# Last projection in four column tiles, last half inverse copied inside SBUF, at most two map loads in flight

## The chip, the cores and the metric

The kernel runs on one core of a Trainium2 chip. The metric is the time in microseconds (us) of one execution on the device; a kernel's time is the median of several executions. A profiled execution is one of them that the hardware profiler recorded, and runs a little longer.

## The reference, cut to what matters

The input x is 64 images of 64 x 64 points. A Fourier neural operator turns them into token maps, and one transformer block follows.

```python
h = concat([x, gx, gy]); v = h @ p_w + p_b             # 32 channels, 64 images, 64 x 64 points
for i in range(4):
    x_ft = rfft2(v)                                    # 24 kx (low and high) x 12 ky are kept
    out1 = einsum('bixy,ioxy->boxy', x_ft[:, :, :12, :12], W1)
    out2 = einsum('bixy,ioxy->boxy', x_ft[:, :, -12:, :12], W2)
    v = irfft2(modes of out1, out2) + conv1x1(v, w_w[i]) + w_b[i]
    v = batchnorm(v) * bn_g[i] + bn_b[i]               # over all images and points
    if i < 3: v = relu(v)
h = v @ q_w + q_b                                      # 64 x 64 tokens x 64 features
h = concat([cls_tok, h])                               # 65 tokens
h = h + attn(layernorm(h))                             # linear attention, 8 heads of 8, norms of k and v
h = h + moe(layernorm(h))                              # 8 experts, top 2
```

## The kernel before, in words

Four images are a quad; 16 quads make the batch. The work before the change's place is three passes over the quads (layers 0 to 2). A pass of layer l computes each quad's output map (`out_set`, L1620), stores it in `maps_d` or keeps it, and already transforms it for the next layer (`y_transform`, `x_transform`; L1678, L1690). Between the passes lies `mix(l)`: TensorE multiplies the kept modes with the layer's complex weights, six weight tiles of which GpSimd loads (L1243) and half negates (L1249) at the start of the mixing; ScalarE copies and squares the products, VectorE sums them for the batch norm.

The last layer has no pass of its own. The last batch norm and the projection `q_w` are linear, so its output is projected at once. The output of the projection, 64 images of 64 x 64, is the sum of two parts, and both are accumulated in PSUM banks 0 to 3 on TensorE:

- the *stream*: for each quad a map of 128 partitions x 4096 (2 MB) of layer 2's output, multiplied by a 128 x 32 matrix cut out of `placed` (L1752): eight matmuls of 512 columns, each recorded twice. The quads come in the order `CONSUMED`; k counts them. k = 0 and 1 are still in SBUF (`KEPT`), the other fourteen are loaded from DRAM by SP (`stream_load`, L1211) into seven buffers (`slot(k)`). `fin_full` counts the maps that have been consumed; it frees the buffers for k = 7 and up. k = 2 and 3 are loaded into the buffers that the pass read its inputs from, k = 4 into the tile `turned`, k = 5 and 6 over the modes.
- the *last inverse transform*: after `mix(3)` the modes are projected with `mode_q` (L1720, L1725), copied to SBUF by ScalarE (L1468, L1470), written to DRAM and read back in another layout by GpSimd (L1326, L1331, L1337; `kl_in`), and transformed along x by TensorE after map k = 3 (L1763). ScalarE copies the result to `x_last` (L1473; `xl_ev`). GpSimd stores `x_last` to the DRAM tensor `line_d` (L1342; `xl_st`), and GpSimd and ScalarE load it back with four transfers each as `g_last` (`last_tile`, L1099; `gl_in`). `last_inverse(c)` (L1740) multiplies it into the banks.

The batch is in two halves, c = 0 for quads 0 to 7 and c = 1 for quads 8 to 15. A half's lines lie at partitions 64 h + 32 c of all four banks, so one map's matmuls alternate between two groups of 32 output columns, 64 h apart. The first eight maps consumed are c = 0. After k = `EARLY` = 9 TensorE waits for both `gl_in` and does `last_inverse(0)`, then the rest of the stream, then `last_inverse(1)`.

Behind it ScalarE evacuates the first half in eight pieces (L1480; `bank_ev`), GpSimd stores it to `tok_d` (`store_lines`, L397) and loads it back with tokens on partitions (`group_load`, L403; `tok_st`). VectorE then works through the first norms of this group (`first_norms(1)`, L682 to L708). ScalarE takes the roots in it (`first_root`, L428, L431; roots 0 and 1 are those of the class token, 2 and 3 those of the first group), and evacuates the second half only after root 3 (L1487). SP stores and loads that half. VectorE's chain of first group, second group, second norms, router, experts and TensorE's matmuls between them then goes to the end.

Every engine and each DMA queue works in the order written: SP's queue, ScalarE's and GpSimd's take an instruction only when the wait before it is met.

Of the kernel before, what the change touches and what calls it, by code (L numbers as in the profile page):

```python
# [6 lines left out]
KX_HALF, KY = 12, 12  # L7
# [105 lines left out]
def tower_kernel(nc, images, p_rows, p_cols, mode_w, conv_w, conv_t, layer_cols, q_cols, cls_tok, head_rows,  # L113
# [13 lines left out]
    line_d = dram("projected_half", [KY, 2, 4, 16, BATCH])  # L127
# [3 lines left out]
    with ctx:  # L131
# [113 lines left out]
        gtile = [t.rearrange("p (x n) -> p x n", x=16) for t in (take(2048), *xhalf[0:2])]  # L245
# [42 lines left out]
        kl_in, xl_full, xl_ev, xl_st, gl_in = sem("kl_in"), sem("xl_full"), sem("xl_ev"), sem("xl_st"), sems("gl_in")  # L288
# [197 lines left out]
        def tensor_tokens(pe):  # L486
# [36 lines left out]
            pe.wait_ge(bank_ev, 12)  # L523
# [592 lines left out]
        def _(sp):  # L1116
# [85 lines left out]

            for l in range(PASSES):
# [6 lines left out]
            def stream_load(k):  # L1210
                sp.dma_start(stream[slot(k)], maps_d[PASSES - 1, CONSUMED[k]]).then_inc(stream_in[slot(k)], 16)  # L1211

            for s in range(2):
                sp.wait_ge(map_st[s], stores(PASSES, 0))
            for pair in range(2):
                sp.wait_ge(a_full[pair], PER_PASS * PASSES)
            stream_load(2)
            stream_load(3)

            sp.wait_ge(x2_ev, mode_of(LAYERS - 1, 6) + 1)  # L1220
            stream_load(4)
# [10 lines left out]
            sp.wait_ge(bank_ev, 12)  # L1232
            store_lines(sp, 1)
            sp.wait_ge(line_st[1], 32)
# [6 lines left out]
        def _(pool):  # L1241
# [107 lines left out]
            pool.wait_ge(line_st[0], 32)  # L1349
# [6 lines left out]
        def _(act):  # L1356
# [128 lines left out]
            for g in range(4):  # L1485
                act.wait_ge(bank_full, g + 5)
# [660 lines left out]
```

## Time and profile before

| | us |
|---|---|
| runs | 1375.55, 1375.92, 1376.15 (median 1375.92) |
| profiled execution | 1386.14 |
| its span, first to last instruction | 1384.3 |
| mean granted TensorE clock | 0.920 of full speed |
| TensorE busy | 1146.5 (83%) |
| VectorE busy | 855.8 (62%) |
| ScalarE busy | 552.4 (40%) |
| GpSimd busy | 365.1 (26%) |

The span is cut by stage rather than by engine: the stream and the last inverse lie between 1160 and 1226, the tokens' chain after that. Times in rows are us from the span's start. A line of a DMA transfer in a queue (SPq, ACTq, POOL with DMA_DIRECT2D) is its issue; the landing comes later.

### The profile page before, as it was taken

What the parts mean: (1) busy time and instruction counts of PE and PEld (TensorE: products, weight loads), DVE (VectorE), ACT (ScalarE), POOL (GpSimd) and SP (SyncE); (2) the same over time, 40 slices, a digit from 0 to 9 for tenths busy, and PEclk for the clock granted to TensorE, in tenths of its full rate; (3) what the DMA queues carried; (4) which work ended last, traced back from release to release, by engine and by line L of the source; (5) the groups of instructions that cost most, each with busy time, mean ns of one, the idle gap of its engine ahead of it and who ended that gap; (6) DMA issues with size and microseconds to landing.
All of it is one profiled execution on the core that took longest, in us unless ns stands there. A gap on an engine that the chain in (4) does not pass through costs nothing.

```text
span 1384.3 us, 40498 instructions
## 1 busy us (share of the span) xinstructions
PE 1146.5 (83%) x18183; PEld 656.8 (47%) x18183; DVE 855.8 (62%) x1033; ACT 552.4 (40%) x808; POOL 365.1 (26%) x525
## 2 busy tenths in 40 slices
PE   3659899999969899899896989889899767954697
PEld 3434555555544455555454445445455452323552
DVE  6547566777648566676664857656666661058664
ACT  2136344445436434344443654434344462100150
POOL 6384212121336301212123730121212261100000
PEclk9779799999989999999998999999999989976788
DMA  6268998898517899999981789999999176931001
GB/s 161 53 185 223 250 271 210 212 226 207 141 46 199 219 331 347 311 353 326 334 248 36 204 217 347 326 317 334 306 338 291 23 269 240 388 119 37 2 0 31
DMA packets 154711, 300.29 MB, mean 217 GB/s; under 512 B 32552, under 2 KB 98488, under 8 KB 137604
## 3 DMA queue, kind: packets, MB, share of 16 engines
q1 hardware_dynamic: 131418, 251.63, 60.2%
q0 software_dynamic: 20864, 45.32, 11.7%
q8 instruction: 143, 2.34, 0.7%
q10 hardware_dynamic: 2256, 0.75, 0.2%
q14 instruction: 30, 0.25, 0.1%
HBM read 147.86 MB, written 128.48 MB: 200 GB/s over the span
## 4 chain that ended last, share of the span: by engine, by line
PE 55%; DMA 16%; DVE 12%; ACT 5%; issue 5%; SPq 4%; POOL 2%; ACTq 0%; DVEq 0%; POOLq 0%
PE ps L1616 13%; PE ps L1655 11%; DMA inputs<-maps 7%; PE ps L1678 6%; PE ps L1690 6%; PE ps L1641 4%; PE ps L1579 3%; PE ps L1543 3%; DMA half_inverse<-arena 2%; PE ps L1558 1%; PE ps L1529 1%; SPq L1053 1%; ACT arena L1427 1%; PE ps L624 1%; DMA arena<-arena 1%
## 5 line engine op out<-in xcount | busy, mean ns | idle before, releaser
L1655 PEld LDWEIGHTS ps<-arena 48*128 48x128 f32 x3072 | 191.2, 197 | 84.6 <-issue 84.6
L1655 PE MATMUL ps<-arena 48*128 48x128 f32 x3072 | 211.6, 289 | 5.0 <-issue 2.9
L1427 ACT ACTIVATE arena<-ps,arena 128x1024 f32<-128x1024 f32 x96 | 112.3, 1202 | 229.8 <-PE ps L1655 208.0
L1094 POOL DMA_DIRECT2D arena<-arena x207 | 120.9, 591 | 304.2 <-ACT arena L1444 300.9
L1436 ACT ACTIVATE ps<-ps 128x1024 f32<-128x1024 f32 x144 | 145.5, 1011 | 111.1 <-PE ps L1616 110.9
L2067 DVE STREAM_TRANSPOSE arena<-ps 128x1024 f32<-128x1024 f32 x96 | 177.3, 1929 | 2.2 <-PE ps L1678 2.2
L1616 PE MATMUL ps<-arena 32*32 32x512 f32 x2944 | 158.5, 620 | 8.0 <-issue 4.9
L1678 PE MATMUL ps<-arena 32*32 32x512 f32 x3072 | 152.8, 616 | 8.0 <-issue 4.6
L2054 DVE STREAM_TRANSPOSE arena<-arena 128x2048 f32<-128x2048 f32 x64 | 144.4, 2289 | 18.6 <-issue 10.0
L1690 PE MATMUL ps<-arena 128*64 128x96 f32 x2304 | 123.4, 258 | 33.4 <-DVE arena L2067 27.8
L1690 PEld LDWEIGHTS ps<-arena 128*64 128x64 f32 x2304 | 103.9, 142 | 89.0 <-issue 51.1
L1249 POOL TENSOR_SCALAR arena<-arena 32x384 f32<-32x384 f32 x96 | 112.9, 1176 | 83.6 <-DMA arena<-in_mode_w 77.3
L2029 DVE TENSOR_SCALAR arena<-ps,arena 128x1024 f32<-128x1024 f32 x32 | 43.0, 1344 | 128.4 <-PE ps L1655 128.4
L1616 PE MATMUL ps<-inputs,arena 32*32 32x512 f32 x1920 | 106.2, 613 | 16.5 <-DMA inputs<-maps 8.5
L1543 PE MATMUL ps<-arena 64*64 64x64 f32 x2304 | 79.7, 287 | 42.4 <-DMA arena<-arena 39.1
L1543 PEld LDWEIGHTS ps<-arena 64*64 64x64 f32 x2304 | 65.1, 154 | 91.8 <-issue 78.6
L1427 ACT ACTIVATE inputs<-ps,arena 128x1024 f32<-128x1024 f32 x48 | 56.1, 1202 | 117.8 <-PE ps L1655 95.5
L1243 POOL DMA_DIRECT2D arena<-in_mode_w x48 | 27.2, 573 | 267.8 <-ACT arena L1444 257.0
L2038 DVE BATCH_NORM_STATS2 arena<-ps 128x6 f32<-128x512 f32 x96 | 62.3, 690 | 43.7 <-PE ps L1616 43.7
L2054 DVE STREAM_TRANSPOSE arena<-inputs 128x2048 f32<-128x2048 f32 x32 | 72.7, 2313 | 8.2 <-issue 4.0
L1034 ACT COPY arena<-ps 128x1024 f32<-128x1024 f32 x66 | 56.2, 857 | 51.4 <-PE ps L1579 51.4
L1616 PEld LDWEIGHTS ps<-arena 32*32 32x32 f32 x2944 | 39.4, 104 | 77.7 <-ACT arena L1427 28.4
(314 smaller groups left out, 1393.9 us busy)
## 6 DMA issues: line engine op xcount, KB each, us to landing
arena<-half_inverse SPq DMA_DIRECT2D x90, 384.0 KB, 12.1
half_inverse<-arena SPq DMA_DIRECT2D x120, 256.0 KB, 4.5
maps<-arena SPq DMA_DIRECT2D x112, 256.0 KB, 4.5
maps<-inputs SPq DMA_DIRECT2D x112, 256.0 KB, 10.2
arena<-maps SPq DMA_DIRECT2D x28, 1024.0 KB, 16.0
maps<-arena SPq DMA_DIRECT2D x28, 1024.0 KB, 19.1
inputs<-maps SPq DMA_DIRECT2D x28, 1024.0 KB, 25.3
arena<-in_mode_w POOLq DMA_DIRECT2D x48, 384.0 KB, 7.2
```

The lines of the kernel that those rows point to most:

```text
L1094: eng.dma_start(dst, src).then_inc((modes_st[batch % 2], last_st, late_st)[part], 16)
L1249: nc.gpsimd.tensor_scalar(w, w, -1.0, None, ALU.mult).then_inc(signed, 1)
L1427: nc.scalar.activation(half(h_out(l, q), h)[:, 1024 * pair:1024 * pair + 1024], ps[:, 2 * pair:2 * pair + 2, :].rearrange("p b n -> p (b n ...
L1436: nc.scalar.activation(src, src, ACT.Square, accum_out=sums_x2[:, i:i + 1])\
L1543: last = nc.tensor.matmul(ps[64 * e:64 * e + 64, 2 * s + m, 0:384] .rearrange("p (b k) -> p k b", b=BATCH)[:, k], ring[2 * p + e][rows, 6 ...
L1616: last = nc.tensor.matmul(ps[32 * x:32 * x + 32, r, :], w[rows, 32 * r:32 * r + 32], source[rows, at:at + 512], start=True, stop=last_one)
L1655: last = nc.tensor.matmul(ps[:, b, at:at + 128], gtile[s][rows, 4 * b + 2 * h + n, :], iy[rows, :], start=False, stop=(i >= 2 and n == 1))
L1678: last = nc.tensor.matmul(ps[32 * x:32 * x + 32, 4 + r, :], fyt[rows, yh, :], src, start=(yh == 0), stop=(yh == 1))
L1690: last = nc.tensor.matmul(ps[64 * t:64 * t + 64, 4 + b, 96 * (y - 3 * b):96 * (y - 3 * b) + 96], spectra[:, at:at + 64], fx2[:, r, :], sta ...
L2038: last = nc.vector.bn_stats(stats[:, 12 * q + 6 * b:12 * q + 6 * b + 6], ps[:, 2 + b, :])
L2054: nc.vector.transpose(dst, src).then_inc(h_turned, 1)
L2067: nc.vector.transpose(dst, src).then_inc(y_turned, 1)
```

## The change

The stream and the last inverse change, and the order of loads on SP. No other function changes.

- `line_of(c, g, h)` gives each of a half's eight lines one of four groups of 32 output columns and one of two banks: half 0 uses banks 0 and 1, half 1 banks 2 and 3. A map's eight matmuls now rotate over four column groups. The evacuation of a half is two instructions of 128 partitions; the store of a half is four transfers for two. The second half is evacuated after roots 0 and 1 and before roots 2 and 3.
- `line_d` is gone. `last_tile` copies from `x_last` to `g_last` directly: twelve transfers for t = 0 from GpSimd and twelve for t = 1 from ScalarE, each of 64 partitions x 64 numbers to 4 partitions x 1024.
- L1763's transform is done after map k = 5 (was 3), and `last_inverse(0)` after k = 10 (was 9).
- Map loads k = 2, 3 and 4 are issued in the last pass, as soon as their buffers are free, before SP's share of the copies of the spectra (`place_part`). The scratch tile of the last mixing moves from `turned` to a tile of its own to make room. From k = 7 on a load also waits until the load two before it has landed.

```diff
-            for h in range(2):
-                rows = slice(64 * h + 32 * c, 64 * h + 32 * c + 32)
-                eng.dma_start(tok_d[32 * c:32 * c + 32, h:8:2, :], lines[rows].rearrange("p (g n) -> p g n", g=4))\
+            for r in range(4):
+                eng.dma_start(tok_d[32 * c:32 * c + 32, r:8:4, :],
+                              lines[32 * r:32 * r + 32, 1024 * c:1024 * c + 1024].rearrange("p (g n) -> p g n", g=2))\
                    .then_inc(line_st[c], 16)
...
-        EARLY = 9
+        EARLY = 10
...
+        def line_of(c, g, h):
+
+            at = 32 * (2 * (g % 2) + h)
+            return slice(at, at + 32), 2 * c + g // 2
...
         def last_tile(eng, t):
 
-            for r in range(4):
-                eng.dma_start(g_last[64 * t + r:64 * t + 4 * KY:4], line_d[:, t, r]).then_inc(gl_in[t], 16)
+            eng.wait_ge(xl_ev, 1)
+            for ky in range(KY):
+                row, at = 64 * t + 4 * ky, 64 * (KYH * (ky % 2) + ky // 2)
+                eng.dma_start(g_last[row:row + 4].rearrange("r g b -> r (g b)").rearrange("r (g b) -> r g b", g=16),
+                              x_last[64 * t:64 * t + 64, at:at + 64]).then_inc(gl_in[t], 16)
...
+                if l == PASSES - 1:
+                    for s in range(2):
+                        sp.wait_ge(map_st[s], stores(PASSES, 0))
+                    for k in range(KEPT, 4):
+                        for pair in range(2):
+                            sp.wait_ge(a_full[pair], set_of(l, "out", QUADS - 4 + k, 1) + 1)
+                        stream_load(k)
+                    sp.wait_ge(y_full, QUADS * PASSES)
+                    stream_load(4)
                 sp.wait_ge(xs_ev, 2 * QUADS * (l + 1))
                 place_part(sp, l, LAST, 2, 2, 1)
...
             for k in range(7, QUADS):
                 sp.wait_ge(fin_full, k - 6 if k < 11 else k - 5)
+                sp.wait_ge(stream_in[slot(k - 2)], streamed(k - 2))
                 stream_load(k)
...
-            pool.wait_ge(xl_ev, 1)
-            for e in range(2):
-                pool.dma_start(line_d.rearrange("(y e) t r g b -> e (t r g) y b", e=2)[e],
-                               x_last[:, 384 * e:384 * e + 384].rearrange("p (y b) -> p y b", b=BATCH))\
-                    .then_inc(xl_st, 16)
-            pool.wait_ge(xl_st, 32)
             last_tile(pool, 0)
-            pool.wait_ge(bank_ev, 8)
+            pool.wait_ge(bank_ev, 2)
             store_lines(pool, 0)
...
-            act.wait_ge(xl_st, 32)
             last_tile(act, 1)
             act.wait_ge(q_read, 2)
-            for g in range(4):
-                act.wait_ge(bank_full, g + 1)
-                for rows in (slice(0, 32), slice(64, 96)):
-                    nc.scalar.activation(lines[rows, 512 * g:512 * g + 512], ps[rows, g, :], ACT.Identity,
-                                         bias=qbias[rows]).then_inc(bank_ev, 1)
-            for i in range(4):
+            for c in range(2):
+                act.wait_ge(bank_full, c + 1)
+                for b in (2 * c, 2 * c + 1):
+                    nc.scalar.activation(lines[:, 512 * b:512 * b + 512], ps[:, b, :], ACT.Identity, bias=qbias)\
+                        .then_inc(bank_ev, 1)
+                if c == 0:
+                    for i in range(2):
+                        first_root(act, i)
+            for i in range(2, 4):
                 first_root(act, i)
-            act.wait_ge(line_st[0], 32)
-            ...
...
-                        b = 64 * h + 32 * (q // 8)
-                        last = nc.tensor.matmul(ps[b:b + 32, g, :], placed[:, 60 - 4 * (q % 8):92 - 4 * (q % 8)],
+                        rows, b = line_of(q // 8, g, h)
+                        last = nc.tensor.matmul(ps[rows, b, :], placed[:, 60 - 4 * (q % 8):92 - 4 * (q % 8)],
                                                 stream[slot(k)][:, at:at + 512], start=(k % 8 == 0), stop=False)
                 last.then_inc(fin_full, 1)
-                if k == 3:
+                if k == 5:
...
-                tile = spectra if l < PASSES else turned
+                tile = spectra if l < PASSES else last_scratch
```

`last_inverse(c)` does the same 32 matmuls, in two turns of 16 for four of 8, with its outputs placed by `line_of`.

## Rows read from the trace of the kernel before

**Rows 1.** Chain of waits, 1176 to 1232: start us, us, what; a DMA piece is the flight.

```profile
1177.22 1.57 PE ps L1763 x4
...
1180.68 0.81 ACT arena L1473
...
1182.64 7.25 DMA projected_half<-arena
...
1192.02 0.75 ACTq L1099
...
1192.79 8.70 DMA arena<-projected_half
...
1201.63 1.55 PE ps L1740 x48
...
1203.26 0.68 ACT arena L1480
...
1209.15 0.54 POOL token_maps L397
1209.69 10.04 DMA token_maps<-arena
...
1220.59 0.84 POOL arena L403
1221.42 4.28 DMA arena<-token_maps
...
1229.71 1.23 DVE arena L686
```

**Rows 2.** Timeline, PE: start us, us, engine line op out<-in xcount [idle before <-releaser].

```profile
1159.90 0.62 PE L1752 MATMUL ps<-arena 128*32 128x512 f32 x1
...
1180.57 17.07 PE L1752 MATMUL ps<-arena 128*32 128x512 f32 x80
```

**Rows 3.** Windows: stretch, us, PE PEld DVE ACT POOL busy, PEclk, DMA share, GB/s.

```profile
1110.00:1112.00 2.00, 0.00 (x0) 0.00 (x0) 0.00 (x0) 0.00 (x0) 0.64 (x2) 0.50 0.80 169
1165.00:1175.00 10.00, 9.66 (x44) 2.62 (x41) 0.00 (x0) 0.00 (x0) 2.39 (x4) 1.00 0.98 325
1205.00:1215.00 10.00, 10.00 (x48) 2.68 (x46) 3.23 (x16) 4.24 (x8) 1.11 (x2) 1.00 1.01 427
```

**Rows 4.** Timeline, weight loads of L1720 at full clock (four column groups).

```profile
1156.43 0.12 PEld L1720 LDWEIGHTS ps<-arena 128*32 128x32 f32 x4 [0.35 <-issue]
1156.86 0.12 PEld L1720 LDWEIGHTS ps<-arena 128*32 128x32 f32 x4 [0.31 <-issue]
```

**Rows 5.** Line L1243 (weights), landing times: layer 2's mixing, then layer 3's.

```profile
DMA to landing us min/median/max: 4.7/6.2/7.2
...
DMA to landing us min/median/max: 9.2/14.0/15.0
```

**Rows 6.** Timeline, PE, mixing of layer 3.

```profile
1129.97 1.54 PE L1543 MATMUL ps<-arena 64*64 64x64 f32 x48 [1.97 <-POOL arena L1249]
```

**Rows 7.** Landing times of L397; L1094 at 200 to 370; L1094 at 900 to 1060.

```profile
DMA to landing us min/median/max: 3.5/6.5/10.0
...
DMA to landing us min/median/max: 5.7/6.1/7.5
...
DMA to landing us min/median/max: 7.1/11.9/21.0
```

**Rows 8.** DMA queues (packets, MB, share): 1209:1220 twice, 1247.5:1253, 1189.8:1202 (ScalarE's).

```profile
q1 hardware_dynamic: 244, 3.47, 74.2%
q0 software_dynamic: 160, 0.52, 11.7%
...
q1 hardware_dynamic: 2383, 0.78, 69.5%
...
q10 hardware_dynamic: 96, 0.20, 4.6%
```

**Rows 9.** Line L1211 (map loads), landing times.

```profile
DMA to landing us min/median/max: 7.9/11.9/18.8
```

More of the change, by code:

```diff
@@ L242, in tower_kernel @@
         stats = take(12 * QUADS)
-        gtile = [t.rearrange("p (x n) -> p x n", x=16) for t in (take(2048), *xhalf[0:2])]
+        last_scratch = take(2048)
+        gtile = [t.rearrange("p (x n) -> p x n", x=16) for t in (last_scratch, *xhalf[0:2])]
         x_pair = [view(at, 4096).rearrange("p (e n) -> p e n", e=2)
@@ L287, in tower_kernel @@
         xl_real = sem("xl_real")
-        kl_in, xl_full, xl_ev, xl_st, gl_in = sem("kl_in"), sem("xl_full"), sem("xl_ev"), sem("xl_st"), sems("gl_in")
+        kl_in, xl_full, xl_ev, gl_in = sem("kl_in"), sem("xl_full"), sem("xl_ev"), sems("gl_in")
         stream_in, fin_full = sems("stream_in", 7), sem("fin_full")
@@ L1201, in layer_pass, with stream_load @@
                         g_load(l, i + 3)
+            def stream_load(k):
+                sp.dma_start(stream[slot(k)], maps_d[PASSES - 1, CONSUMED[k]]).then_inc(stream_in[slot(k)], 16)
             for l in range(PASSES):
@@ L1205, in _ @@
                 layer_pass(l)
+                if l == PASSES - 1:
[7 more added lines that the diff above has]
+                    stream_load(4)
                 sp.wait_ge(xs_ev, 2 * QUADS * (l + 1))
                 place_part(sp, l, LAST, 2, 2, 1)
[L1210 to L1221, printed above, removed]
             sp.wait_ge(x2_full, mode_of(LAYERS - 1, KY - 1) + 1)
@@ L1231, in _ @@
             sp.wait_ge(fin_full, QUADS)
-            sp.wait_ge(bank_ev, 12)
+            sp.wait_ge(bank_ev, 4)
             store_lines(sp, 1)
-            sp.wait_ge(line_st[1], 32)
+            sp.wait_ge(line_st[1], 64)
             group_load(sp, 1)
@@ L1473, in _ @@
             nc.scalar.copy(x_last.rearrange("p (b n) -> p b n", b=2), ps[:, 5:7, 0:384]).then_inc(xl_ev, 1)
-            act.wait_ge(xl_st, 32)
             last_tile(act, 1)
             act.wait_ge(q_read, 2)
-            for g in range(4):
-                act.wait_ge(bank_full, g + 1)
-                for rows in (slice(0, 32), slice(64, 96)):
-                    nc.scalar.activation(lines[rows, 512 * g:512 * g + 512], ps[rows, g, :], ACT.Identity,
-                                         bias=qbias[rows]).then_inc(bank_ev, 1)
-            for i in range(4):
-                first_root(act, i)
-            act.wait_ge(line_st[0], 32)
-            for g in range(4):
-                act.wait_ge(bank_full, g + 5)
-                nc.scalar.activation(lines[:, 512 * g:512 * g + 512], ps[:, g, :], ACT.Identity, bias=qbias)\
-                    .then_inc(bank_ev, 1)
+            for c in range(2):
[7 more added lines that the diff above has]
+            for i in range(2, 4):
+                first_root(act, i)
             scalar_tokens(act)
@@ L1730, in last_inverse @@
             def last_inverse(c):
-                for i, turn in enumerate(TURNS):
-                    if i >= 2:
-                        pe.wait_ge(turn_done, 4 * QUADS * PASSES + 2 * c + i - 1)
+                for turn in range(2):
+                    if turn:
+                        pe.wait_ge(turn_done, 4 * QUADS * PASSES + c + 1)
                     for n in range(2):
-                        for half_x, g in turn:
-                            rows = slice(64 * half_x, 64 * half_x + 48)
-                            at = 256 * n + 128 * half_x
+                        for low in range(2):
                             for h in range(2):
-                                b = 64 * h + 32 * c
-                                last = nc.tensor.matmul(ps[b:b + 32, g, at:at + 128],
-                                                        g_last[rows, 4 * g + 2 * h + n, 32 * c:32 * c + 32],
-                                                        iy[rows, :], start=False, stop=(i >= 2 and n == 1))
-                    last.then_inc(bank_full if i >= 2 else turn_done, 2 if i >= 2 else 1)
+                                for half_x in range(2):
+                                    g = 2 * ((turn + half_x) % 2) + low
+                                    rows = slice(64 * half_x, 64 * half_x + 48)
+                                    at = 256 * n + 128 * half_x
+                                    line, b = line_of(c, g, h)
+                                    last = nc.tensor.matmul(ps[line, b, at:at + 128],
+                                                            g_last[rows, 4 * g + 2 * h + n, 32 * c:32 * c + 32],
+                                                            iy[rows, :], start=False, stop=(turn == 1 and n == 1))
+                    last.then_inc(bank_full if turn else turn_done, 1)
             for k, q in enumerate(CONSUMED):
@@ L1769, in _ @@
                     for t in range(2):
-                        pe.wait_ge(gl_in[t], 64)
+                        pe.wait_ge(gl_in[t], 16 * KY)
                     last_inverse(0)
```

5 lines of the change are left out of this document (2 added, 3 removed).

## The prediction

> **What bounds the kernel now.** I read the chain of waits over the end of the program first. The reader is to see that the last third of it does not hang on matmuls: it is one chain of small transfers [rows 1]. TensorE transforms the last spectra (L1763), ScalarE copies them out, GpSimd stores them in DRAM, and the 256-byte pieces come back by eight transfers (L1099; ScalarE's last lands at 1201.49). Then come the last inverse of the first half (L1740), eight evacuations, a store of the token maps and their load; VectorE starts the first group's norms at 1225.7. From there VectorE's own chain leads to the end, so the change is worth what it does to 1225.7 plus whatever holds VectorE later.
>
> TensorE's row over the same stretch looks like a bound but is none: 80 records (five maps of 16) in 17.07 us, 3.4 us a map, back to back [rows 2]. The second half's maps are evacuated only after ScalarE's root for the first group, at 1239, so TensorE's end at 1226.2 has 13 us of room. The transfers of the maps are the other busy resource: 427 GB/s with all DMA engines full; 2.10 MB / 427 = 4.9 us a map [rows 3].
>
> **The change part by part.** Times below are of the profiled execution, whose span of 1384.3 lies in 1386.14; the runs shown have a median of 1375.92, so I add the difference in us to that.
>
> *Column tiles.* Before, a map's eight matmuls alternate between two column groups and go at 2 records per 0.43 us (17.07/80 = 0.213 each). L1720 rotates over four groups with the same shape and goes at 4 records per 0.43 us [rows 2, 4]. So a map costs 1.7 us, not 3.4; the bounds are 1.7 and 3.4. Sixteen maps save 27 us of TensorE, off the path. What is late next is the transfers: nine maps (k=7 to 15) must be loaded after the first is consumed.
>
> *Maps 2 to 4 loaded earlier.* They go out at about 1075 to 1097, into idle DMA engines, not at 1111.7 beside the weights of the last mixing. The weights' landings were 9.2 to 15.0 us there and 4.7 to 7.2 us one layer earlier [rows 5], without that company. GpSimd's sign flips then start some 4 us earlier, and TensorE's waits for them go: 1.97 us [rows 6] and a second of 0.8. ScalarE (2.4 us a mode) and VectorE take over; following them mode by mode I get 1.4 us (bounds 0 and 2.8). SP's six small transfers now stand behind three loads, which have landed by 1104 and the copies start at 1107: nothing. The scratch tile moved away costs nothing.
>
> *Until the last transform.* The stream starts at 1159.9 - 1.4 = 1158.5, the first map is consumed at 1160.6 and the first load flows from 1161.8, some 3 us earlier than before. It meets GpSimd's stores of the projected modes, and I let that eat the 1.4: L1763 again at 1177.2 (bounds 1175.5 and 1179). TensorE has then been idle since about 1169, though, and such a gap leaves the granted clock at 0.50, the 1.2 GHz level [rows 3]; 3.4 us of transform become some 5.2. The copy (0.8) ends at 1183.3.
>
> *The half inverse copied on the chip.* Removed: L1342 and its 7.25 us, then eight gathers. Added: 12 transfers of 64 pieces of 256 bytes on GpSimd and 12 on ScalarE. Issue alone: 12 x 0.75 = 9.0 us on ScalarE [rows 1], to 1192.3. If they landed as the quickest transfer of the token maps does, 3.5 us after its issue [rows 7], they would be in at 1196, 5 us before 1201.5. But they run beside the loads, for which the nearest rows say three things. (a) L397's 160 packets from GpSimd are 10 on each of 16 engines, and took 0.54 + 10.04 = 10.6 us beside the loads, where the same store from SP on idle engines took 3.5 and some more (I take 4.2) [rows 1, 7, 8]: 6.4 us for 10 packets, 0.64 a packet, which is the time of one 16 KB packet of a load (3.47 MB in 244 packets with the completions; 16.4 KB at 427/16 GB/s = 0.61 us). So each packet of another queue waits for one packet of the loads, whatever its size. (b) L1094's identical copies land in 5.7 to 7.5 us in the first layer's pass and 7.1 to 21.0 in the third, where the transfers beside them have longer rows [rows 7]. (c) GpSimd's queue gathers pieces (0.52 MB in 160 packets), a sequencer's hardware queue does not: the token gather of 256-byte pieces made 2383 packets of 0.78 MB. And ScalarE's 4 transfers of L1099, 12 outer rows each, made 96 packets: 12 of data and 12 completions each, so as many engines as outer rows [rows 8]. The new ones write 4 rows: by that pattern 4 engines, with 16 + 1 packets per transfer on each, 12 x 17 = 204. At 0.64 us that is 130 us as long as loads flow; when they end, packets of that queue go at 0.026 us (69.5% of 16 engines over 5.5 us, by 2383 [rows 8]).
>
> So the copies land shortly after the loads end. Loads: 1161.8 + 9 x 4.9 = 1205.9; plus 3 for the gather of the projected modes (325 in place of 427 GB/s over ten us [rows 3] is 2.4) and 2 for the copies themselves: 1211 (bounds 1206 and 1214). By then (1211 - 1187) / 0.64 = 38 of 204 packets are through, 166 x 0.026 = 4.3 are left, and with the completion gl_in is there at 1216. GpSimd's twelve, gathered, are in at about 1198 and don't decide.
>
> The page "DMA: Bandwidth & Descriptors" of the Trainium skill says in "Queues, rings and completion order" that an engine takes turns between queues packet by packet, with 9 to 17 descriptors typical in a packet. Here ScalarE's and SP's small packets were one piece each (330 bytes on average), so (c) decides over "typical"; what it would give otherwise is the third rival.
>
> *Limit of two loads.* A load waits for the one two before it; with one still queued behind, SP's queue runs dry nowhere (a load lands 7.9 us after its issue at the least, 4.9 of them its own flow [rows 9]). The copies meet the same row of 16 KB packets: nothing; bounds -1 and +2 us on the loads' end. Behind that wait on SP stands only cls_tok, which is not due.
>
> *After the copies.* TensorE has waited since about 1191, its clock is low: last_inverse(0) 1.6 becomes 3.2. Evacuation: 2 of 0.68 for 8, saving 4.1 us. Four stores for two: 0.3 + 3 x 0.55 until the last goes out, then 4.2 us, since the loads are over, in place of 10.04. Load: 0.3 + 0.84 + 4.3. Sum 0.1 + 3.2 + 1.4 + 0.3 + 1.65 + 4.2 + 0.3 + 0.84 + 4.3 = 16.3, so VectorE starts at 1216 + 16.3 = 1232.3, 6.6 us later than 1225.7.
>
> *ScalarE's order.* Roots 2 and 3 now stand behind the second half's evacuation. TensorE does k=11 to 15 and the inverse from 1219.3: 5 x 1.7 + 1.8 cold + 2 = 1231.6, evacuated at 1233. VectorE wants root 2 at its start + 5.2 [rows 1] = 1237.5: hidden, 4 us to spare. Behind VectorE's start nothing changes.
>
> **Forecast: 1375.9 + 6.6 = 1382.5 us.** Own range 1377 to 1388.
>
> **Rivals.**
> 1. *The copies get through beside the loads* (many small packets per turn). gl_in at 1197 to 1199 (issue end plus the landing of GpSimd's); inverse and evacuation to 1203; last store out 1205, 8 to 10 us beside loads: 1214; load to 1219.5, root 2 in time. 6 us earlier plus up to 2: 1368. For it: a 256-byte packet occupies an engine for hardly anything; against it: the completions in (a) are 4-byte packets and count as full turns.
> 2. *Turns, but the loads end early or the copies spread over 16 engines* (12 x 5 = 60 packets, 22 left at 1211): gl_in at 1212, VectorE 2.6 later: 1378; with the loads ending at 1207, 1374.5 to 1376. Same or barely slower. For it: ends of my bounds; against: the 12-engine pattern.
> 3. *ScalarE's queue packs 16 pieces into a packet, as GpSimd's does* [rows 8]: 12 x 2 = 24 turns x 0.64 = 15 us and 3 to begin: gl_in 1202, store out 1209, beside the last loads 6 us, load: 1220.5, so 1371.
> 4. *The column tiles bring nothing* (3.4 us a map): the loads then follow TensorE as before, ending near 1215 to 1218, and root 2 waits behind the second half: 1384 to 1390.
>
> **Chances.** Forecast 0.40; rival 1 0.25; rival 2 0.20; rival 3 0.10; rival 4 0.05. Range for 8 in 10: 1366 to 1387. A measurement tells about 0.2% (2.75 us) from no change. Faster (below 1373.2): rivals 1 and 3 and little else, 0.36. Same: most of rival 2 and the lower end of the forecast, 0.20. Slower: 0.44.
>
> **What would show it.** Right: L1752 at about 0.11 us a record with TensorE idle between maps; ScalarE's copies issued in 9 us but landing more than 15 us after their last issue, together with the end of the maps' transfers; the chain of waits with one long DMA piece from ScalarE's copies to L1740. Its queue should hold about 816 packets (12 x 68) in that stretch. Wrong: L1740 of the first half before 1200 means turns don't cost what I say; 960 packets mean 16 engines; a wait of VectorE for ScalarE's L428 of several us means that the second half's evacuation stands in the way; records of L1752 still 0.21 apart refute the first part.

## The result, and the profile after

The kernel after takes 1387.03 us (median of 4 runs, 1385.08 to 1387.49), the kernel before 1375.74 beside it; the ratio is 1.0077, 95% interval 1.0042 to 1.0112. Taken again on another occasion the same kernel gave 1.0066 [1.0030, 1.0103]. Ratios leave out executions that ran over 1.5% above the fastest of their kernel.

It is slower, as forecast and by the forecast mechanism, but by more than the 6.6 us forecast: the medians differ by 11.3 us, and 1387.03 lies above the 1382.5 forecast, at the upper end of the forecast's own range of 1377 to 1388 and just over the one given for 8 in 10, to 1387. The profiled execution took 1385.08 us with a span of 1383.2; it is the shortest of the four, where that of before, 1386.14, is longer than all of its runs.

The spans of two profiled executions can't be subtracted here: before's own span (1384.3) is longer than after's. What is compared below is counted from the first matmul of the last mixing, which is at 1113.43 in before and at 1105.81 in after.

The chain of waits of after (start us, us, what), which answers to [rows 1]:

```profile
1153.43 6.92 DMA projected_modes<-arena
...
1171.44 2.94 PE ps L1764 x4
...
1177.38 0.81 ACT arena L1475
1178.21 1.13 ACTq L1106
...
1182.98 5.58 ACTq L1106
...
1188.59 7.34 ACTq L1106
...
1197.14 16.11 DMA arena<-arena
...
1213.39 1.18 PE ps L1741 x32
...
1215.88 1.27 ACT arena L1481 x2
...
1217.44 1.54 POOL token_maps L396 x3
1218.98 2.71 DMA token_maps<-arena
...
1222.81 4.75 DMA arena<-token_maps
1227.59 1.23 DVE arena L682
```

From the copy of the transform's result (L1475) to the last inverse (L1741) it is 36.0 us: of ScalarE's twelve issues two stall ahead of the last, for 5.58 and 7.34 us, and the last copy lands 16.11 us after its issue began. In [rows 1] the same way, by DRAM, ended at 1201.63, 21 us after its copy began (in the second trace of before, c1, 23.2 us). Behind it the chain is quick: store 2.71 us (10.04 before), since no load is left to run beside it.

TensorE over the same stretch, answering to [rows 2], with ScalarE's issues between (start us, us, engine line op out<-in xcount [idle before <-releaser]):

```profile
1150.77 3.57 PE L1753 MATMUL ps<-arena 128*32 128x512 f32 x28
1153.79 0.60 PE L1753 MATMUL ps<-inputs,arena 128*32 128x512 f32 x2
...
1171.44 5.90 PE L1764 MATMUL ps<-arena 24*128 24x384 f32 x8 [9.80 <-DMA arena<-projected_modes]
...
1178.21 24.73 ACTq L1106 DMA_DIRECT2D arena<-arena  x12
...
1213.39 2.33 PE L1741 MATMUL ps<-arena 48*32 48x128 f32 x64 [25.64 <-DMA arena<-arena]
```

28 records start between 1150.77 and 1153.79, 0.108 us apart at full clock, against 0.211 by the same measure in before (80 between 1180.57 and 1197.48): the column tiles work. The maps of one stretch run back to back, as the window shows (columns as in [rows 3]):

```profile
1155.00:1160.00 5.00, 5.00 (x52) 1.63 (x48) 0.00 (x0) 0.00 (x0) 0.00 (x0) 1.00 0.85 293
```

TensorE's idle time lies ahead of the transform (9.80 us) and of the last inverse (25.64 us). All twelve issues of ScalarE together take 24.73 us.

DMA queues between 1178 and 1214 (packets, MB, share of 16 engines), and the landing times of all fourteen map loads (L1212) and of the weights (L1251) in the last mixing, to [rows 8], [rows 9] and [rows 5]:

```profile
q1 hardware_dynamic: 782, 10.48, 83.6%
q10 hardware_dynamic: 816, 0.20, 3.5%
q0 software_dynamic: 384, 0.21, 2.7%
...
DMA to landing us min/median/max: 7.6/11.1/15.3
...
DMA to landing us min/median/max: 3.2/5.9/7.6
```

ScalarE's queue (q10) holds 816 packets, 12 x 68, as the prediction had it: four engines. The nine loads issued between 1150 and 1215 land in 9.8 to 15.3 us. The weights land in 5.9 us at the median in place of 14.0.

The places in us from the start of the last mixing, from the timelines. "Transform" is the start of L1763 or its equal, "inverse" that of `last_inverse(0)`, VE1 and VE2 the starts of VectorE's first and second group (L682, 128 x 1024), and the last column is the ratio of the times to before, with its 95% interval:

```
kernel                  transform inverse  VE1    VE2    end    ratio
before                     63.8    88.2   112.3  140.0  270.9
c1 before, again           64.6    91.0   114.7  141.2  272.3  1.0032 [1.0000, 1.0063]
after                      65.6   107.6   121.8  149.4  277.4  1.0077 [1.0042, 1.0112]
a1 after, again            69.4   107.2   121.2  148.9  277.0  1.0066 [1.0030, 1.0103]
a2 load 11 held            63.1    80.8   112.2  143.0  273.9  1.0029 [0.9987, 1.0072]
a3 no limit of two         66.6   106.2   120.1  147.9  278.4  1.0045 [1.0000, 1.0090]
a4 column tiles only       67.7    90.2   113.8  139.9  268.2  1.0000 [0.9958, 1.0042]
b1 way by DRAM             63.5    93.0   110.7  138.2  266.4  0.9973 [0.9938, 1.0008]
b2 DRAM, load 10 held      62.8    79.2   114.0  140.1  268.6  0.9974 [0.9941, 1.0007]
b3 copies, load 10 held    65.9    82.5   116.3  142.5  270.7  0.9983 [0.9946, 1.0019]
b4 24 copies on GpSimd     63.4   108.2   122.6  150.4  280.1  1.0054 [1.0018, 1.0090]
c2 early loads only        63.3    89.9   112.9  140.7  269.2  0.9983 [0.9952, 1.0014]
c3 one queue               65.9    82.2    97.4  132.4  260.5  0.9911 [0.9875, 0.9946]
d1 loads in 4 KB pieces    61.8   109.7   123.8  151.6  281.3  1.0075 [1.0040, 1.0110]
```

Before against itself (c1) reads 1.0032, so a ratio alone settles no 3 us; two traces of one kernel agree in these columns to 3 us, but for the transform of a1, which is 3.8 us later than in after. The trace of a4 is of its longest execution, 1391.89 us, where its median is 1374.70.

### The profile page after: what moved, and what is told of

The parts are those of the page before. It is cut to its first block, busy times and chain, and to the rows that moved or that the text cites. A ratio compares the mean times of both kernels' runs of the same rounds, so it can differ in the third digit from the quotient of the medians.

```text
span 1383.2 us, 40517 instructions
## 1 busy us (share of the span) xinstructions
PE 1118.7 (81%) x18183; PEld 645.4 (47%) x18183; DVE 855.6 (62%) x1033; ACT 546.5 (40%) x800; POOL 370.3 (27%) x533
## 4 chain that ended last, share of the span: by engine, by line
PE 59%; DVE 12%; DMA 9%; SPq 6%; ACT 5%; issue 5%; ACTq 1%; POOL 1%; DVEq 0%
PE ps L1615 14%; PE ps L1654 11%; PE ps L1677 7%; PE ps L1689 6%; PE ps L1578 4%; PE ps L1640 3%; PE ps L1542 3%; SPq L1162 2%; DMA arena<-arena 2%; PE ps L1557 2%; DMA arena<-maps 2%; PE ps L1528 1%; ACTq L1106 1%; ACT arena L1429 1%; DVE ps L1907 1%
## 5 line engine op out<-in xcount | busy, mean ns | idle before, releaser
L1654 PEld LDWEIGHTS ps<-arena 48*128 48x128 f32 x3072 | 184.8, 192 | 92.5 <-issue 87.0
L1654 PE MATMUL ps<-arena 48*128 48x128 f32 x3072 | 204.7, 283 | 12.8 <-issue 6.8
L1429 ACT ACTIVATE arena<-ps,arena 128x1024 f32<-128x1024 f32 x96 | 112.3, 1202 | 226.0 <-PE ps L1654 207.4
L1615 PE MATMUL ps<-arena 32*32 32x512 f32 x2944 | 157.3, 624 | 10.0 <-DMA arena<-maps 6.3
L1677 PE MATMUL ps<-arena 32*32 32x512 f32 x3072 | 150.5, 612 | 5.4 <-DVE arena L2055 3.4
L1689 PE MATMUL ps<-arena 128*64 128x96 f32 x2304 | 126.6, 261 | 32.8 <-DVE arena L2068 28.7
L1689 PEld LDWEIGHTS ps<-arena 128*64 128x64 f32 x2304 | 106.7, 145 | 89.9 <-issue 50.7
L1615 PE MATMUL ps<-inputs,arena 32*32 32x512 f32 x1920 | 110.0, 634 | 5.7 <-issue 4.6
L1429 ACT ACTIVATE inputs<-ps,arena 128x1024 f32<-128x1024 f32 x48 | 56.1, 1202 | 119.1 <-PE ps L1654 101.2
L1251 POOL DMA_DIRECT2D arena<-in_mode_w x48 | 27.3, 582 | 262.6 <-ACT arena L1446 252.2
```

What stands on the lines that cost most here:

```text
L1429: nc.scalar.activation(half(h_out(l, q), h)[:, 1024 * pair:1024 * pair + 1024], ps[:, 2 * pair:2 * pair + 2, :].rearrange("p b n -> p (b n ...
L1615: last = nc.tensor.matmul(ps[32 * x:32 * x + 32, r, :], w[rows, 32 * r:32 * r + 32], source[rows, at:at + 512], start=True, stop=last_one)
L1654: last = nc.tensor.matmul(ps[:, b, at:at + 128], gtile[s][rows, 4 * b + 2 * h + n, :], iy[rows, :], start=False, stop=(i >= 2 and n == 1))
L1677: last = nc.tensor.matmul(ps[32 * x:32 * x + 32, 4 + r, :], fyt[rows, yh, :], src, start=(yh == 0), stop=(yh == 1))
L1689: last = nc.tensor.matmul(ps[64 * t:64 * t + 64, 4 + b, 96 * (y - 3 * b):96 * (y - 3 * b) + 96], spectra[:, at:at + 64], fx2[:, r, :], sta ...
```

## The experiments

**a1, after again; a2, the loads held.** a1 is the kernel after unchanged; in a2 SP waits for both `gl_in` before load k=11:

```diff
                 sp.wait_ge(stream_in[slot(k - 2)], streamed(k - 2))
+                if k == 11:
+                    for t in range(2):
+                        sp.wait_ge(gl_in[t], 16 * KY)
```

> The changed kernel once more, beside the runs of before on the same chip, so that the other kernels of this call have their reference. Theory (A: ScalarE's one-piece packets each take a turn with the 16 KB packets of the map loads): 1387 us, first L1741 about 107 us after the first L1542 of the last mixing, as in its first trace (1213.4 - 1105.8), with a wait of some 25 us of TensorE before it. Rival (B: the 11 us lie elsewhere, in noise of the passes): 1376 to 1390 with the tail as before.

> The changed kernel, but SP issues no map load from k = 11 on until both halves of g_last have landed. Theory A: with the load of k = 10 through by about 1182 the copies drain at once; gl_in some 3 us after ScalarE's last issue, at 1190 on the clock of the first trace in place of 1213; the loads of k = 11 to 15 follow from there and end at 1217 (5 x 4.9 plus the store beside them); the store of the first half now runs beside loads (10 us for 4), VectorE starts at 1213 to 1216 in place of 1227.6, root 2 waits 1 to 3 us for the second half: 1373 to 1377 us. Rival B' (24 small transfers are slow by themselves, by their issue and their landing): gl_in no earlier than 1205, the loads end 25 us after it, 1387 us or more.

a1 repeats after to 1 us from the inverse on; its median is 1380.67 us, where I had 1387, with before at 1374.31 beside it. In a2 none of ScalarE's issues stalls (7.62 us for the twelve) and the last copy is in 3.70 us after its issue; then the loads go on. From its chain, and VectorE's wait behind it:

```profile
1176.97 0.56 ACTq L1108
1177.56 3.70 DMA arena<-arena
...
1181.35 8.06 DMA arena<-maps
...
1219.91 1.27 ACT arena L1486 x2
...
1221.40 0.25 DVE L688 RECIPROCAL arena<-arena 128x16 f32<-128x16 f32 x1 [3.38 <-ACT arena L428]
```

The inverse starts 11.7 us after the start of ScalarE's copy (1169.67 to 1181.40), where it was 36.0, so what the copies waited for was the loads. The ratio, 1.0029, separates neither from 1.0 nor from after's: the loads now fall on the first half's stores, and ScalarE's root for VectorE stands behind the second half's late evacuation (L1486), for which VectorE waits 3.38 us. Of what I expected, the inverse came sooner (80.8 from the mixing, where 1190 in after's trace is 84.2), VectorE's start later (112.2, for 107 to 110), and the median of 1379.86 us is above my 1373 to 1377.

**a3, no limit of two.**

```diff
-                sp.wait_ge(stream_in[slot(k - 2)], streamed(k - 2))
```

> The changed kernel without the wait for the load two before. In the trace of the change ScalarE's queue passed most packets in three or four bursts, where SP's queue ran dry between two loads. Theory A: without the limit the queue does not run dry, the bursts go, and ScalarE's copies wait for the end of the loads, which comes 2 to 3 us earlier: gl_in within 3 us of the changed kernel's, 1385 to 1389 us; in a window inside the loads ScalarE's queue makes fewer than 8 packets a us. Rival C (the limit itself costs load time and so the 11 us): 1378 to 1382.

Places within 2 us of after's. The median is 1377.83 us, not the 1385 to 1389 that I expected but the number of rival C; a1, unchanged, has 1380.67 beside it, and the two ratios lie within each other's intervals, so the time doesn't decide between theory and rival. What decides is the inverse at 106.2, no earlier than after's by more than 1.4 us. The queues between 1180 and 1200, a stretch without a burst of q10, and then between 1201 and 1206, where the loads are over:

```profile
q1 hardware_dynamic: 484, 7.11, 97.1%
q0 software_dynamic: 261, 0.14, 2.9%
q10 hardware_dynamic: 118, 0.03, 0.6%
...
q10 hardware_dynamic: 510, 0.12, 13.1%
q1 hardware_dynamic: 21, 0.20, 9.9%
```

118 packets in 20 us on four engines are 4 x 20 / 118 = 0.68 us for each, about the time of one packet of the loads' queue (16 x 20 / 484 = 0.66 us, completions counted with it). 510 of the 816 are left when the loads end, and then take under 5 us. This is the turn of the prediction, measured.

**a4, the column tiles alone.** On before: `line_of`, the new order of `last_inverse`, two evacuations and four stores a half; way by DRAM, loads and EARLY as before.

```diff
-                        b = 64 * h + 32 * (q // 8)
-                        last = nc.tensor.matmul(ps[b:b + 32, g, :], ...
+                        rows, b = line_of(q // 8, g, h)
+                        last = nc.tensor.matmul(ps[rows, b, :], ...
```

> The kernel before with the column tiles alone: line_of, four column groups, two evacuations per half, four stores per half; projected_half in DRAM, the order of the loads, k = 3 and EARLY = 9 and the order of the roots as before. Theory A: L1752 goes at 0.107 us a record, the loads of k = 7 to 10 are issued 2 to 6 us earlier and meet the stores and the gather of the projected modes (+2 to +4), the transform L1763 is at the low clock (+2), the evacuation saves 4: 1375 to 1380 us, so at most a third of the 11 us. Rival D (the column tiles, by starting the loads earlier and cooling TensorE's clock, cost most of it): 1383 or more.

1.0000 [0.9958, 1.0042]: the column tiles with their shorter evacuation show no change by themselves, though the interval can't exclude one of up to 5.8 us either way; VectorE starts at 113.8 (112.3 and 114.7 in before). That rules out rival D, which wanted 1383 us or more; the median is 1374.70.

**b1, the way by DRAM put back.** The reverse cut: after with `line_d`, GpSimd's two stores and 4 + 4 gathers of before; all else stays.

```diff
-            eng.wait_ge(xl_ev, 1)
-            for ky in range(KY):
-                ...
-                eng.dma_start(g_last[row:row + 4]..., x_last[64 * t:64 * t + 64, at:at + 64]).then_inc(gl_in[t], 16)
+            for r in range(4):
+                eng.dma_start(g_last[64 * t + r:64 * t + 4 * KY:4], line_d[:, t, r]).then_inc(gl_in[t], 16)
```

> The kernel after, with the way of the half inverse put back as before (two stores to line_d by GpSimd, then 4 + 4 gathers of 12 x 16 pieces by GpSimd and ScalarE); column tiles, early loads, limit of two and the order of the roots stay. Theory A (the 24 copies are the whole loss, 816 packets of 256 bytes that go one by one beside 16 KB packets): the time from the transform L_x (L1764) to the first last_inverse falls from 42 us to 24 to 28 us as before, VectorE's start of the first group from 121 to 105 to 110 us after the third mixing's start; against the kernel before the total is then lower by what the column tiles' shorter path (before to VectorE's start: some 4 us) and the early loads bring: ratio 0.995 to 0.999. Rival B (the early loads and the limit of two, or the 5.9 us of cold transform, carry a part of the loss): VectorE's start stays 3 us or more behind before's 112 and the ratio above 1.000.

```profile
1170.81 10.49 DMA projected_half<-arena
1181.58 1.54 POOL arena L1107 x3
1183.11 9.48 DMA arena<-projected_half
```

From the start of ScalarE's copy to the inverse the way by DRAM takes 23.8 us beside the same loads (1168.85 to 1192.68; 21.0 and 23.2 in the two traces of before, 36.0 by the copies); VectorE starts at 110.7, 11 us before after, and the ratio falls from 1.0077 and 1.0066 to 0.9973 [0.9938, 1.0008]. The copies are the whole loss; the rest of the change brings VectorE's start 1.6 to 4.0 us forward, which the ratio can't tell from nothing. The inverse is 29.5 us behind the transform's start, above the 24 to 28 expected: the transform itself is 2.2 us longer than before's, the store 3.2.

**b2 and b3, loads held, with either way.** Both hold load k=10 until `gl_in`, set EARLY to 7, and let ScalarE do the four roots ahead of the second evacuation; b2 goes by DRAM, b3 keeps the 24 copies.

```diff
-        EARLY = 10
+        EARLY = 7
...
+                if k == 10:
+                    for t in range(2):
+                        sp.wait_ge(gl_in[t], GL)
...
                 if c == 0:
-                    for i in range(2):
+                    for i in range(4):
                         first_root(act, i)
```

> As b1, and three things more: SP holds the load of map k=10 until the half inverse is in place, the first half's inverse follows map 7 instead of 10, and ScalarE does all four roots of the first group before the second half's evacuation. Theory A (each packet of another queue waits for a 16 KB packet as long as loads flow): bounce in 12 to 14 us after the copy (24 before), VectorE's start at 100 to 106 us after the third mixing's start; the second group's at 128 to 134 (140 before), so 6 to 12 us below before: ratio 0.991 to 0.996. Rival (loads held back come late and the second half is what VectorE waits for): second group not before 138, ratio 0.998 to 1.002.

> The kernel after with the three things of b2 (load k=10 held until the copies are in, first half's inverse after map 7, roots first). Theory A: with no load beside them the 24 copies land within 2 to 4 us after their last issue (11 us after the copy in an earlier run with load 11 held), so gl_in comes at 80 to 82 us after the third mixing's start, VectorE's start 102 to 108, second group 130 to 136; ratio 0.992 to 0.998, within 2 us of b2: the bounce by DRAM costs about as much as issuing twelve copies. Rival (copies on the chip are worth their issue only on idle queues of the chip, and ScalarE's issue of 12 stands in the way of the evacuation): 3 us or more behind b2.

b2's chain, then b3's, then b2's again behind the inverse, where VectorE's start (L683) ends it:

```profile
1167.18 3.06 DMA projected_half<-arena
1170.27 1.30 ACTq L1107
1173.12 2.38 DMA arena<-projected_half
```

```profile
1173.60 0.56 ACTq L1108
...
1174.18 2.68 DMA arena<-arena
...
1177.00 1.18 PE ps L1744 x32
```

```profile
1180.85 12.74 DMA token_maps<-arena
1195.30 15.08 DMA arena<-token_maps
1210.40 1.23 DVE arena L683
```

Beside no load the two ways cost the same: from the end of ScalarE's copy to the inverse 9.6 us by DRAM (1166.03 to 1175.6) and 9.9 by the 24 copies (1167.10 to 1177.00). Copying on the chip saves a store and a gather's latency and gives it back in twelve issues. My expectation for VectorE's start (100 to 108) missed: the loads that were released at the inverse fell on the token maps' store (12.74 us, 2.71 in after) and load (15.08, 4.75 in after). The gain had only been moved along the chain. The rest of my numbers missed with it: the second groups start at 140.1 and 142.5, where I had 128 to 134 and 130 to 136, and the ratios, 0.9974 and 0.9983, are above my ranges (0.991 to 0.996, 0.992 to 0.998). b2's rival had the second group right, but not the reason: it comes 26 us behind the first in both, no more than in before (27.7 and 26.5), so it is the first group that was late.

**b4, all copies on GpSimd.**

```diff
             last_tile(pool, 0)
+            last_tile(pool, 1)
...
-            last_tile(act, 1)
```

> The kernel after with all 24 copies on GpSimd, none on ScalarE. Theory A (turns): a copy of GpSimd's takes about 2 turns on each of 16 engines beside the loads; 24 x 2 x 0.64 = 31 us from 1178, so gl_in comes some 3 to 6 us before after's (104 to 110 us after the third mixing's start) and VectorE's start at 116 to 119; ratio to before 1.000 to 1.006. Rival (the fault is ScalarE's queue of one-piece packets on 4 engines alone; GpSimd's are cheap): gl_in at 95 to 99, VectorE's start at 108 to 112, no slower than before.

```profile
1171.20 14.13 POOL arena L1106 x23
1185.33 23.84 DMA arena<-arena
```

The inverse is at 108.2, no better than after's 107.6. So it isn't ScalarE's queue with its one-piece packets on four engines alone: GpSimd's, with 32 packets a copy on 16 engines (384 for twelve in after) in place of 68 on four, needs as long for 24, and the rival fell. Between 1190 and 1200 GpSimd's queue has 229 packets and the loads' 220, one for one on the same 16 engines, or 0.70 us for each of GpSimd's: the turn again. By turns I had 31 us from the start; measured are 38 (1171.20 to 1209.17), and only then does TensorE go on; VectorE starts at 122.6, later than my 116 to 119.

**c1 and c2, before again and the early loads alone.** c2 is before with SP's part of after for maps 2 to 4 (and the scratch tile moved).

```diff
+                if l == PASSES - 1:
+                    ...
+                        stream_load(k)
+                    sp.wait_ge(y_full, QUADS * PASSES)
+                    stream_load(4)
                 sp.wait_ge(xs_ev, 2 * QUADS * (l + 1))
```

> The kernel before once more, for a second trace. If what is counted from the start of the third mixing is repeatable (theory), VectorE's start of the first group lies again at 112 to 113.5 us from it, the second group's at 140, the end at 268 to 271, whatever the start itself is (1100 to 1120 into the span); ratio 1.000.

> The kernel before with the loads of maps 2 to 4 ahead of the last copies of SP, and nothing else of the change. Theory: the mixing's end comes 1.5 to 2 us earlier (mode_q's matmul at 37 us from the mixing's start, 39 before), but the maps are still consumed at 3.4 us each and their loads follow TensorE, so VectorE's start comes 0 to 2 us earlier: ratio 0.998 to 1.000. Rival: the whole 2 us reach VectorE and the loads of half 1 end earlier too: ratio 0.996 to 0.998.

c1 lies 1 to 3 us over before in each column, VE1 at 114.7 and the end at 272.3 just outside what I wrote. In c2 the first matmul with `mode_q` is at 37.2 (39.0 and 38.4 in before), so the mixing is 1.2 to 1.8 us shorter; 0.9983 [0.9952, 1.0014] can't tell that from nothing.

**c3, no load beside any small transfer.** b2 with load 11 (not 10) held, and the first half's stores and load taken from GpSimd's queue into SP's, ahead of loads 12 to 15:

```diff
+                if k == 11:
+                    for t in range(2):
+                        sp.wait_ge(gl_in[t], GL)
+                if k == 12:
+                    sp.wait_ge(bank_ev, 2)
+                    store_lines(sp, 0)
+                    sp.wait_ge(line_st[0], 64)
+                    group_load(sp, 0)
...
-            pool.wait_ge(bank_ev, 2)
-            store_lines(pool, 0)
-            pool.wait_ge(line_st[0], 64)
-            group_load(pool, 0)
```

> The kernel of b2 (way by DRAM, first inverse after map 7, roots first) with load k=11 held until the half inverse is in place, and the first half's stores and load of token maps put into SP's own queue ahead of loads 12 to 15, so that no load runs beside them. Theory A (a small packet costs one turn of a 16 KB packet only where loads flow): the stores land in 3 to 5 us after the last issue (12.7 in b2), the load of the token maps in 4 to 6 (15.1 in b2), VectorE's start at 94 to 98 us from the third mixing's start (114 in b2, 112 before), and then the second half decides: its tokens land at 126 to 131, so VectorE's second group starts there, 9 to 14 us before before's 140; ratio 0.990 to 0.995. Rival (the loads held back come later than that): second group at 138 or later, ratio 0.997 to 1.000, and VectorE idle for 10 us or more ahead of it.

Its chain, and VectorE's waits for the two groups:

```profile
1180.37 3.07 DMA projected_half<-arena
...
1194.53 4.22 DMA token_maps<-arena
...
1201.10 12.99 DMA arena<-maps
1214.14 9.71 DMA inputs<-maps
...
1203.94 1.22 DVE L683 TENSOR_REDUCE arena<-arena 128x16 f32<-128x1024 f32 x1 [7.29 <-DMA arena<-token_maps]
...
1238.99 1.22 DVE L683 TENSOR_REDUCE arena<-arena 128x16 f32<-128x1024 f32 x1 [1.64 <-DMA arena<-token_maps]
```

0.9911 [0.9875, 0.9946], median 1366.84 us (before 1376.21 beside it): this version beats both kernels. VectorE starts its first group 15 us before before's place and its second 8 us before. The second half, held back behind the pauses, now decides, at 132.4 where I expected 126 to 131.

**d1, the loads in 4 KB pieces.** The turn itself: same bytes, but each map load as four transfers of 128 x 1024.

```diff
-                sp.dma_start(stream[slot(k)], maps_d[PASSES - 1, CONSUMED[k]]).then_inc(stream_in[slot(k)], 16)
+                for j in range(4):
+                    at = slice(POSITIONS // 4 * j, POSITIONS // 4 * (j + 1))
+                    sp.dma_start(stream[slot(k)][:, at], maps_d[PASSES - 1, CONSUMED[k]][:, at])\
+                        .then_inc(stream_in[slot(k)], 16)
```

> The kernel after with each load of a last map (k=2 to 15) written as four transfers of 128 x 1024, so that its pieces and packets are 4 KB in place of 16 KB; the bytes, the limit of two maps and all else stay. Theory A (a small packet of another queue waits for one packet of the loads, so a turn costs 0.16 us here in place of 0.64): 204 packets an engine take at most 33 us and fewer where the queue of SP runs dry, and GpSimd's copies take a quarter: the half inverse is in place 22 to 33 us after its copy (36 in after), 12 to 1 us before the loads end, its issue on ScalarE stalls less (under 5 us in all, 11 in after), VectorE's start 106 to 119 us after the third mixing's start (122), ratio 1.000 to 1.005. Rival (what a small packet waits for has a time of its own, whatever the loads' pieces are): copies in place 35 us after their issue or later, with the end of the loads, ratio 1.006 or more.

Queues between 1180 and 1195:

```profile
q1 hardware_dynamic: 1477, 5.39, 98.6%
q10 hardware_dynamic: 359, 0.09, 2.6%
```

4 x 15 / 359 = 0.167 us for a small packet, and 16 x 15 / 1477 = 0.162 us for one of the loads: with packets of a quarter the turn is a quarter (0.68 in a3). So theory A holds for what a small packet waits for. Its number for the outcome fell, though, and the rival's stood: the inverse came at 109.7 and the ratio is 1.0075. 204 packets at 0.167 are 34 us, about what I had given as the most; the bursts between loads that I had counted on for fewer didn't come (18 to 25 packets a us in each 5 us from 1165 to 1195). The issue on ScalarE stalled as in after, 23.87 us for the twelve, where I had under 5 us of stalls.

## Why the prediction was right, and where it was not

*What bounds the kernel.* Right: the chain of small transfers ahead of VectorE sets the end. The five kernels in which the inverse comes at 106 to 110 have the five highest ratios (1.0045 to 1.0077), and the stream's matmuls show no worth by themselves (a4, 1.0000 within 0.0042).

*Column tiles.* Right: 0.108 a record at full clock for 0.11, off the path. The idle time between maps that I had named as a sign didn't come; TensorE stands idle ahead of the transform and of the inverse.

*Early loads.* Right: `mode_q` starts at 36.99 and 37.17 in after and a1, at 39.03 and 38.42 in before and c1, 1.2 to 2.0 us for 1.4, with the weights' landings as the reason.

*L1763 at the same time.* It came 2 us later (65.6, and 69.4 in a1, for 63.8): the stores of the projected modes took 6.92 us for 2.78, so in this trace their contention ate more than the 1.4. It doesn't always: nine kernels are the same up to this place but for the limit of two in a3, and have it at 62.8 to 69.4, with the same stores at 2.74 us in b1 and 7.17 in c3. Forecasting no change was right within that scatter. I had bounds of 1175.5 to 1179 for it, which are 62.1 to 65.6 from the mixing. The cold transform is 5.90 for 5.2. The window of it (columns as in [rows 3]) has the clock at the 1.2 GHz level, after 9.80 us of idle TensorE:

```profile
1171.00:1177.00 6.00, 5.50 (x8) 2.32 (x8) 0.00 (x0) 0.00 (x0) 0.00 (x0) 0.50 1.00 423
```

*The copies.* The mechanism is shown: small packets wait a load's packet each (a3, b4, d1), the waits vanish when no load flows (a2, b3), and the copies are the whole loss (b1). The step that failed is the one in "Limit of two loads", that SP's queue runs dry nowhere, together with the loads' end at 1211 worked out from 427 GB/s. In after the queues' rows for 1178 to 1183, 1183 to 1185 and 1205 to 1207 are

```profile
q10 hardware_dynamic: 3, 0.00, 0.1%
...
q10 hardware_dynamic: 180, 0.04, 18.5%
...
q10 hardware_dynamic: 252, 0.06, 19.2%
```

and 243 more between 1198 and 1200: 675 of ScalarE's 816 packets went through in three moments of 2 us, not at the end. These are moments in which SP's queue was all but dry. Of the 128 packets of 16 KB of a load, the one before had 22, 4 and 0 left at 1183, 1198 and 1205, and the next had been issued 1.9 to 2.3 us earlier (1180.95, 1196.07, 1202.69); a3 has one such moment as well (150 packets between 1176 and 1178, 9 left at 1176), then 118 packets in 20 us, and 510 at the end. That on the four engines in question the old load was through and the new one not yet there is my reading; the trace doesn't name a packet's engine.

The loads in turn were slower, 10.47 MB between 1178 and 1212 or 308 GB/s, for a reason that no run isolates, and ended at 106 to 107 from the mixing, where I had 1211 or 97.6. The two errors nearly cancel: the inverse at 107.6 for 102.6, 5 us late, and not a drain of 4.3 us behind the loads but under 1. That the forecast of it came so near is in part luck. GpSimd's twelve copies, for which I had 1198 or 84.6, were through at 96, also without effect. The issue on ScalarE, for which I had 9.0 us, took 24.73 (27.08 in a1), with no effect as far as I can see, since the last copies would have waited for the loads anyway; no run tests that.

*Limit of two loads.* Nothing, within the bounds of -1 and +2: a3 is 1 to 2 us earlier at VectorE's start.

*The chain after.* 14.2 us (107.6 to 121.8) for 16.3: the cold inverse took 2.33 for 3.2 and the store 2.71 for 4.2.

*Root 2.* Hidden in after (ScalarE's root for the group waits 4.34 us for VectorE), as forecast; in a2 it was not.

*VectorE's start and behind.* In sum: 121.8 and 121.2, against 112.3 and 114.7, +8.0 on the means, where I had 118.9 (1232.3). Behind it I said nothing changes; before needs 158.6 and 157.7 us from there to the end, after 155.6 and 155.8. So the traces give +5.6 us from the mixing to the end, with 6.6 forecast, at the low end of both intervals (1.0042 and 1.0030 are 5.8 and 4.1 us). The measured ratios give 9 to 11 us. What the rest is, and where the 2.4 us behind VectorE's start come from, stays open; from VE2 to the end traces show 128.0 to 128.5 in eight kernels and 129.7 to 131.1 in six, before among these both times. c2, whose tail is before's, is among the eight, so this part looks like scatter rather than a gain of the change.

The rivals: 1 and 3 needed the inverse before 1200 and fell; so did 4 (0.108 a record). Rival 2's end of the loads was on the wrong side, and the 816 packets mean four engines, not 16. What the Trainium skill says on the page "DMA: Bandwidth & Descriptors", in "Queues, rings and completion order", that engines take turns between queues packet by packet agrees with a3 and d1 (0.68 and 0.167 us a turn); its 9 to 17 descriptors typical in a packet would by my estimate have made 45 to 85 packets of 768 pieces; ScalarE's queue here held 816, one for each piece and completion.

## What to carry to other kernels

Beside a stream of large packets a small transfer paid here per packet, not per byte: count its packets on its busiest engine times the time of one packet of the stream (0.66 us for 16 KB, 0.16 for 4 KB here), completions included, before replacing few gathered pieces by many. When a chain of small transfers sets the end and the stream has slack, hold the stream and put the small ones ahead of it in its own queue (c3, 0.9911); but follow the gain to the last waiter, since holding the stream at one link only moved the cost to the next (b2).

## What the runs showed of the hardware

- A DMA issue can itself stall: of ScalarE's twelve copies of 68 packets the eighth and ninth took 5.58 and 7.34 us to issue (in a1 the ninth and eleventh, 9.05 and 11.24) in place of 0.56; none did where no load flowed (a2, 7.62 us for all twelve).
- Small packets beside no load go fast: 339 of ScalarE's in 3 us in b3 (1170 to 1173), 0.035 us each on four engines, which is the pace of their issue (17 on each engine per copy, 0.59 us apart). Behind the loads in a3, all issued, 406 went in 2 us (1202 to 1204), 0.020 us each. A copy inside SBUF was then no quicker than the way by DRAM (9.9 and 9.6 us).
